# The bias of a graph layer's first product: a rank-two matmul, or a ScalarE copy into the PSUM bank

## The reference

```python
h = jnp.maximum(_layernorm(x, axis=-1), 0.0)
h = h @ W + b_w                      # 1250x512 times 512x512, plus a bias row
s_dst = h @ a[:D_OUT]; s_src = h @ a[D_OUT:]
e = leaky_relu(s_dst[dst] + s_src[src] + b_a)
w = exp(e); alpha = w / segment_sum(w, dst)[dst]
out = segment_sum(alpha[:, None] * h[src], dst)
```

## Time and profile before

| | us |
|---|---|
| three runs | 798.42, 801.49, 803.20 |
| median | 801.49 |
| the profiled execution: its own time | 802.81 |
| its span, first to last instruction | 801.0 |
| PE busy | 763.7 (95%) |
| DVE busy | 396.7 (50%) |
| ACT busy | 274.6 (34%) |
| mean granted TensorE clock | 0.983 |

### The profile page before, as it was taken

The page is one execution under the profiler, slowest core; times in us unless marked ns, Lnnn a source line. Parts: engine busy times, 40 slices in busy tenths (PEclk is TensorE's granted clock), DMA queues, the critical chain, the costliest instruction groups (busy, mean ns, idle before and its releaser), DMA issues.

```text
span 801.0 us, 11770 instructions
## 1 busy us (share of the span) xinstructions
PE 763.7 (95%) x3755; PEld 625.2 (78%) x3755; DVE 396.7 (50%) x981; ACT 274.6 (34%) x567; POOL 120.3 (15%) x134
## 2 busy tenths in 40 slices
PE   5789999999899999999999999899999999999993
PEld 3479978888788887777777777788888888888882
DVE  8888888998642548523525325332233223322320
ACT  6836665565542422312314213121122121211211
POOL 4000000000000102830000000232231332322211
PEclk9989999999899999999999999999999999999998
DMA  9000000312501247799796955599438964449900
GB/s 226 3 2 4 4 2 12 116 63 75 180 1 54 80 136 241 210 344 327 228 368 223 352 192 158 180 268 338 118 75 217 288 235 111 101 120 279 323 11 6
DMA packets 46789, 125.55 MB, mean 157 GB/s; under 512 B 7300, under 2 KB 7432, under 8 KB 46713
## 3 DMA queue, kind: packets, MB, share of 16 engines
q1 hardware_dynamic: 28581, 80.73, 31.2%
q0 software_dynamic: 9488, 26.95, 13.1%
q10 hardware_dynamic: 8644, 16.86, 6.6%
HBM read 72.21 MB, written 53.20 MB: 157 GB/s over the span
## 4 chain that ended last, share of the span: by engine, by line
PE 91%; DVE 3%; ACT 2%; DMA 2%; issue 1%; POOL 0%; DVEq 0%; ACTq 0%; SPq 0%; POOLq 0%
PE ps L1578 17%; PE ps L1579 17%; PE ps L1580 17%; PE ps L1958 6%; PE ps L1957 6%; PE ps L1648 3%; PE ps L1885 3%; PE ps L1823 3%; PE ps L1824 3%; PE ps L1606 1%; PE ps L1929 1%; PE ps L1712 1%; PE ps L1714 1%; PE ps L1713 1%; PE ps L1968 1%; PE ps L1740 1%
## 5 line engine op out<-in xcount | busy, mean ns | idle before, releaser
L1958 PE MATMUL ps<-slots,CTs 125*128 x230 | 90.9, 395 | 0.0
L1957 PE MATMUL ps<-slots,CTs 125*128 x207 | 81.5, 394 | 0.0
L1413 DVE TENSOR_TENSOR he_t<-ps,b_b 125x512 f32<-125x512 f32 x40 | 27.5, 690 | 105.8 <-PE ps L1580 72.9
L1506 DVE CAST CTs<-ps 125x512 fp32r<-125x512 f32 (+1 forms) x69 | 37.2, 595 | 85.0 <-PE ps L1885 85.0
L918 ACT ACTIVATE slots<-he_t 125x512 fp32r<-125x512 f32 x40 | 25.3, 634 | 152.6 <-DVE he_t L1413 148.2
L1551 DVE TENSOR_TENSOR tm<-ps,b_b 128x512 f32<-128x512 f32 x23 | 15.9, 691 | 104.1 <-PE ps L1580 104.1
L643 POOL DMA_INDIRECT out<-tg,rec x23 | 36.9, 1604 | 193.8 <-ACT tg L968 160.4
L1578 PE MATMUL ps<-W,agT_hi 128*125 128x512 f32 x160 | 63.5, 397 | 0.0
L1578 PE MATMUL ps<-W,h2T_hi 128*125 128x512 f32 x160 | 63.4, 396 | 0.0
L1580 PE MATMUL ps<-W,agT_lo 128*125 128x512 f32 x160 | 63.3, 396 | 0.0
L1579 PE MATMUL ps<-W,agT_hi 128*125 128x512 f32 x160 | 63.2, 395 | 0.0
(11 more groups left out here) (301 smaller groups left out, 1718.1 us busy)
## 6 DMA issues: line engine op xcount, KB each, us to landing
he_d<-slots SPq DMA_DIRECT2D x30, 448.0 KB
slots<-he_d SPq DMA_DIRECT2D x30, 448.0 KB
w_d<-slots SPq DMA_DIRECT2D x3, 4096.0 KB, 20.1
slots<-w_d SPq DMA_DIRECT2D x24, 512.0 KB, 23.9
t_d<-he_t SPq DMA_DIRECT2D x40, 224.0 KB
c_d<-c_nat SPq DMA_DIRECT2D x10, 546.9 KB
raw<-in_L_gnn_Wl ACTq DMA_DIRECT2D x4, 1024.0 KB, 8.3
raw<-in_L_gnn_Wr ACTq DMA_DIRECT2D x4, 1024.0 KB, 5.7
```

The costliest lines, as they stand in the source:

```text
L1413: v.tensor_tensor(he_t[:, n % 4, :], ps[0:P, bank_of(x, g, t), :], b1_b[:, x % 2, :], ALU.add).then_inc(pre_ready.sem, 1)
L1506: v.tensor_copy(CTs[:, 4 * r:4 * r + n, :], ps[0:P, r, 0:n * S].rearrange("p (c n) -> p c n", n=S)).then_inc(cts_ready.sem, 1)
L1957: mm(o, CTs[:, t, :], part(k, P, t * 1024, P), start=False, stop=False)
L1958: last = mm(o, CTs[:, t, :], part(k, P, t * 1024 + D, P), start=False, stop=t == T - 1)
```

## The change

- The matmul of `ones_2` with `bw_2` is gone, and with it both tiles, their POOL memsets, ACT's copy of the high part and DVE's subtraction of the low part.
- ACT gets a step `bias_in(b)` in each round, between `turned_high0(b)` and `columns(b+1)`: it copies `bw_b` (125 x 512) into bank 6. In round 0 it waits for the bias's DMA and for `covered`, in the others for `hw_lo_ready(b)`, which is DVE's `nat_lo` of tile b-1, the last reader of the bank.
- The twelve matmuls of the product all add to what is in the bank (`start=False`). PE waits for `bias_ready(b + 1)`.
- PE gets one matmul, `cover_product`, after block 9 of the hot products. It writes all of bank 6 with `start=True`; its values are never read.
- `bw_b` moves to another place in SBUF, since it is now read until round 9.

```diff
-        bw_b = at("bw_b", [P, D], F32, R1 + 4096)
...
-        bw_2 = early("bw_2", [128, D], F32R)
-        ones_2 = early("ones_2", [128, P], F32R)
+        bw_b = early("bw_b", [P, D], F32)
...
-            link(g.memset(f32(bw_2[:]), 0.0))
-            link(g.memset(f32(ones_2[:]), 1.0))
-            pool.sem_inc(small_ready.sem, 1)
...
+            def bias_in(b):
+                if b == 0:
+                    act.wait_ge(*small_in(48))
+                    act.wait_ge(*covered(1))
+                else:
+                    act.wait_ge(*hw_lo_ready(b))
+                copy(ps[0:P, 6, :], bw_b[:]).then_inc(bias_ready.sem, 1)
+
...
-            act.wait_ge(*small_in(48))
-            act.wait_ge(*small_ready(1))
-            copy(bw_2[0:1, :], bw_b[0:1, :]).then_inc(bw_hi_ready.sem, 1)
...
                 turned_high0(b)
+                bias_in(b)
                 if b + 1 < T:
                     columns(b + 1)
...
-                dve.wait_ge(*bw_hi_ready(1))
-                v.tensor_tensor(bw_2[32:33, :], bw_b[0:1, :], f32(bw_2[0:1, :]), ALU.subtract).then_inc(bw_lo_ready.sem, 1)
...
+            def cover_product():
+
+                mm(ps[0:P, 6, :], q_sel[:, 0, :], q_sel[:].rearrange("p c n -> p (c n)")[:, 0:D], start=True, stop=True
+                   ).then_inc(covered.sem, 1)
+
...
+                if u == 9:
+                    cover_product()
...
-                if b > 0:
-                    pe.wait_ge(*hw_lo_ready(b))
-                else:
+                if b == 0:
                     pe.wait_ge(*w0_lo_ready(1))
-                    pe.wait_ge(*bw_lo_ready(1))
+                pe.wait_ge(*bias_ready(b + 1))
                 o = ps[0:P, 6, :]
-                mm(o, ones_2[:], bw_2[:], start=True, stop=False)
                 for c in range(KC):
-                    mm(o, hT_hi[:, c], W0_hi[:, c], start=False, stop=False)
...
+                    mm(o, hT_hi[:, c], W0_hi[:, c], start=False, stop=False, skip_group_check=True)
...
```

More of the change, by code:

```diff
@@ L348, in gnn_kernel @@
          var_ready, std_ready, norm_ready, h_ready, turned, hT_hi_ready, hT_lo_ready, s_done, hw_done,
-         hw_hi_ready, hw_lo_ready, bw_hi_ready, bw_lo_ready, sums_used, small_ready, s_ready, sd_ready, sd_spread, row_ready) = signals(
+         hw_hi_ready, hw_lo_ready, bias_ready, covered, sums_used, s_ready, sd_ready, sd_spread, row_ready) = signals(
              "w0_hi_ready w0_lo_ready wa_f_ready ab_ready wa_ready "
              "var_ready std_ready norm_ready h_ready turned hT_hi_ready hT_lo_ready s_done hw_done "
-             "hw_hi_ready hw_lo_ready bw_hi_ready bw_lo_ready sums_used small_ready s_ready sd_ready sd_spread row_ready")
+             "hw_hi_ready hw_lo_ready bias_ready covered sums_used s_ready sd_ready sd_spread row_ready")
         (low_ready, zl_ready, ze_ready, pf_ready, ph_ready, pl_ready, p_used, summed, den_done, rden_ready, x2_ready,
@@ L1702, in tile_and_batch @@
                     spread(0)
-                if b > 0:
-                    pe.wait_ge(*hw_lo_ready(b))
-                else:
+                if b == 0:
                     pe.wait_ge(*w0_lo_ready(1))
-                    pe.wait_ge(*bw_lo_ready(1))
+                pe.wait_ge(*bias_ready(b + 1))
                 o = ps[0:P, 6, :]
-                mm(o, ones_2[:], bw_2[:], start=True, stop=False)
                 for c in range(KC):
-                    mm(o, hT_hi[:, c], W0_hi[:, c], start=False, stop=False)
-                    mm(o, hT_hi[:, c], W0_lo[:, c], start=False, stop=False)
-                    last = mm(o, hT_lo[:, c], W0_hi[:, c], start=False, stop=c == KC - 1)
+                    mm(o, hT_hi[:, c], W0_hi[:, c], start=False, stop=False, skip_group_check=True)
+                    mm(o, hT_hi[:, c], W0_lo[:, c], start=False, stop=False, skip_group_check=True)
+                    last = mm(o, hT_lo[:, c], W0_hi[:, c], start=False, stop=c == KC - 1, skip_group_check=True)
                 last.then_inc(hw_done.sem, 1)
```

## The result

The changed kernel took 804.76 us (median of 20 runs, 799.88 to 806.67), the kernel before 800.81 us (20 runs, 798.42 to 803.20). The ratio of the means is 1.004, 95% interval 1.0025 to 1.0056, that of the medians 1.0049: slower by 0.4 to 0.5%. That is inside the 0.5% which the forecast took as its mark, though the interval reaches past it. The forecast was +3.65 us and 805.1; the medians differ by 3.95.

A forecast was written before the change was run, and what follows sets the result against it. PE bound the tile stage at 7.02 us per tile; the edit closes a DVE-ACT loop of 7.59, and seven turns from 55.33 end 3.65 us late. Against the median of 801.49 that gives 805.1 us, range 800.5 to 808.5.

The forecast's parts named there:

- PE as the bound, and its two reserves: Ten tiles of `tile_and_batch`: PE sets the 7.02 us period; `column` has 0.4 us to spare, `hT_lo` 0.93.
- The loop's length: Per tile: one-hots, `nat_lo`, ACT's bias copy, `column` and the next one-hots form a closed loop of 7.59 us.
- The removed product: Tiles 1 to 9: the product of ones leaves PE, saving 0.31 us each; PE's own work drops to 6.71.
- rival A: In the tile stage PE stays the bound, loop 6.7 or shorter; 799.5 us, by the median 798.2; chance 0.12.
- Tile 0: First tile: W0 products need no bias split, start at 46.63, last 5.12 us; tile 1 opens at 51.75, 0.83 earlier.
- the cover product's 0.44: After hot block 9: the added PE product makes block 11, and DVE's work through to W0_lo, 0.44 us later.
- Behind tile 9: After the last tile: a DVE and ACT chain, then PE in the attention, pass the 3.65 us delay on.
- The size, 3.65: Tile 9's one-hots at 108.46 instead of 104.81, 3.65 us late, and the attention and the end equally late.
- Signs named ahead: New profile: one-hots every 7.6 us, ACT and PE idle while waiting, tile 1 near 51.8, attention near 123.1.
- B: On ACT the table load is already done when the wait ends; loop 7.40, time 803.6 us; chance 0.10.
- C: In later tiles PE's new pauses of 0.88 us cost the granted clock; time 809 us; chance 0.12.

The follow-up runs named there:

- the run without bias product: The kernel before with the bias left out of the W0 product, along with the split of its low part; 798.04 us, ratio 0.9957.
- the second profile: The changed kernel executed again, unaltered; 802.57 us (one run).
- the first experiments: The first four follow-up kernels, each one edit to the changed kernel or the kernel before; the kernel before, run again beside them, had a median of 800.85 us.
- the run that reads the table first: The changed kernel, with ScalarE reading the table of the columns before it waits for nat_lo and copies the bias; 801.24 us, ratio 1.0006.
- the run with the wait only: The kernel before plus ACT's wait for nat_lo and a copy of the bias onto itself ahead of the columns; 805.41 us, ratio 1.0054.

## Why the prediction was right, point by point

- **PE as the bound, and its two reserves** (step "what bounds the kernel now"): right. `column` had 0.4 us to spare, the wait moved it by more, and the stage changed hands. The waits view now puts 1.42 us before the one-hots down to `column`, where it had named PE for what was the sequencer's own work.
- **The loop's length**, 7.59: right, 7.57, term by term. The bias copy into PSUM took 0.60, the nearer of the two rows I had.
- **The removed product**, 0.31 per tile: mis-sized. It was 0.23, as the run without bias product shows. The forecast did not hang on it, because it was given away to the pauses anyway; rival A's time did. The pauses are 7.57 - 6.79 = 0.78, not 0.88.
- **Tile 0**: W0_lo and the cover product's 0.44 right (0.42), the start at 46.53 for 46.63. But I let the twelve products take 5.12 us, the price at half clock. They took 4.45 at a granted clock of 0.76 from 45 to 52 us, and 2.88 (46.54 to 49.42) in the second profile at 1.00. That is most of why the profiled shift at tile 9 is 2.68 and not 3.65: 55.33 - 54.51 = 0.82 earlier at tile 2, and seven turns of 0.02.
- **Behind tile 9**: the delay does pass through. In the ten profiles the attention starts anywhere between 114.28 and 125.67, and the rest lasts 676.1 to 681.5. It goes with the clock columns: 680.4 to 681.5 where the first reads 0.83 or 0.85, 679.0 to 679.2 at 0.91 and 0.93, 680.8 at 0.91 and 0.86, 676.1 where both read 1.00. It has no trend with the attention's start, so a shift there is, apart from the clock, a shift of the end.
- **The size, 3.65**: the medians say 3.95, and that they come so near is partly luck. The two profiled executions are 2.68 apart at tile 9, 3.15 at the attention and 2.3 at the end. At equal mean clock, with the kernel before taken from the runs beside the first experiments, the changed kernel is 3.4 slower at 0.982 (806.46 against 803.03), 3.5 at 0.984 (805.24 against 801.71), 3.7 at 0.986 (804.34 against 800.68), but 5.0 at 0.989 and 4.7 at 0.991, where there are one to three runs a side. The sum lies in that span; how the 3.95 divides between loop and clock stays open.
- **Signs named ahead**: the period, ACT's wait, the opening of tile 1 within 0.8 and the attention within 0.5 were as said. PE's pause was 0.68 us in tile 3 (its period is 72.03 - 64.56 = 7.47, against 6.79) and 0.78 later, for 0.5 and 0.9. Its idle row was not there: the wait was in a stretched matmul row and in PEld.
- **Rivals**: A is refuted in the changed kernel, and became true once the order on ACT was changed, at 797.05 (I gave it 798.2). Two sizes in it missed and cancelled: tile 1 opened 1.64 earlier, not 0.83, and taking the product away saved 8 x 0.23 = 1.8, not 2.5. B is refuted by the run that reads the table first. A wait of the bias copy did hold back the table load, 82.8 against 82.81. The Trainium skill, "Perfetto Trace Analysis", section "DVE / Act Engine Instruction", has the sequencer fetch on while an instruction waits; for a register load behind a waiting ACTIVATE these traces don't agree. C did not happen at pauses of 0.78 while the loop ran (the clock fell only at the stage's end, from 115.5 to 119 us); at 1.23 it fell in two tiles inside the stage (0.50 from 86 to 89 and from 110 to 112 us), and even that cost the loop nothing. That it was hidden behind DVE's one-hots, as I had worked out for a single slow product, fits the unchanged spacing.

## What to carry to other kernels

A step that is cheap on an idle engine is not free if it waits: ask what stands behind it on that engine, and who makes the thing it waits for. If the two answers meet, a loop has been closed, and its length can be added up from single rows before anything is built. Here the same copy, placed behind the work that others need, turned a loss of 4 us into a gain of 4 by the medians, of which part goes with the clock.

## What the runs showed of the hardware that was not expected

- The same kernel's time follows the mean granted clock closely: the changed kernel took 799.88 at 0.993 and 806.67 at 0.982. A difference of 4 us lies inside that spread, so profiles of one execution each compare best by spacings in a stage and not by their ends.
- The profile can print a waiting PE as busy. The row of the 25 counting products reads 3.42 us for 2.87, and the next row starts 3.40 after it for 2.63: 0.77 us of waiting leave no idle time. From 54 to 110 us PE is printed busy for 55.35 of 56.
- ACT's copy of 125 x 512 took 0.60 us from SBUF to PSUM, 0.63 from SBUF to SBUF in the run with the wait only (its row at 84.31), and pieces of 64 columns into PSUM stood 0.15 us apart.
- The place behind the small products costs the first large matmul 0.09 us more than the following ones, whichever matmul stands there.
